# Joining the half-filled products of a routed feed-forward, and moving steps around its expert tiles

## What is computed

```python
logits = x @ W_router.T                      # 8 experts, top 2 per token
probs = softmax(logits); rw, sel = top_k(probs, 2)
combine = zeros((T, E)).at[arange(T)[:, None], sel].add(rw)
sh = silu_and_mul(x @ Ws_gate_up, 704) @ Ws_down          # shared expert: 256 -> 2*704 -> 256
shared_out = sh * sigmoid(x @ W_sgate.T)
gu = einsum('th,ehi->eti', x, We_gate_up)                 # each expert: 256 -> 2*176
# ... silu_and_mul(gu, 176), then We_down: 176 -> 256, weighted with combine, plus shared_out
```

## Time and profile before

| what | us |
|---|---|
| median of 3 runs (1372.93 to 1376.32) | 1374.88 |
| the profiled execution, its own time | 1379.76 |
| its span, first to last instruction | 1377.8 |
| TensorE busy in the span | 1289.3 (94%) |
| VectorE, ScalarE, GpSimd busy | 888.4, 776.2, 436.3 |
| last stage, from its first instruction at 1161.3 | 216.5 |

### The profile page before, as it was taken

How to read it: one execution, slowest core, us unless ns; L and a number is a source line. 1 busy time by engine, 2 the same in 40 slices (tenths; PEclk the granted TensorE clock), 3 DMA queues, 4 the chain that set the end, 5 groups by cost and what they waited for, 6 DMA issues and landing times. The chain is left out here.

```text
span 1377.8 us, 23715 instructions
## 1 busy us (share of the span) xinstructions
PE 1289.3 (94%) x8242; PEld 1139.5 (83%) x8242; DVE 888.4 (64%) x2436; ACT 776.2 (56%) x2113; POOL 436.3 (32%) x420
## 2 busy tenths in 40 slices
PE   3799999999999879999999988999999998899998
PEld 3588888888888768888888877998988987789986
DVE  4688888888887656643433345667676767585647
ACT  3587777777777623322222257666666665455542
POOL 1365556545654433100000002222241332053430
PEclk8999999999999979999999989999999999899999
DMA  7000000000000400300000020000000024123433
GB/s 251 9 1 1 9 1 0 0 8 0 0 0 1 98 0 1 123 1 0 0 0 1 9 69 9 1 9 1 9 29 4 13 83 115 43 73 102 124 113 136
DMA packets 42771, 49.91 MB, mean 36 GB/s; under 512 B 13711, under 2 KB 35160, under 8 KB 41912
## 3 DMA queue, kind: packets, MB, share of 16 engines
q1 hardware_dynamic: 38888, 38.33, 9.2%
q0 software_dynamic: 3792, 10.40, 2.0%
HBM read 36.23 MB, written 12.49 MB: 35 GB/s over the span
## 5 line engine op out<-in xcount | busy, mean ns | idle before, releaser
L955 POOL TENSOR_TENSOR probs_a<-probs_a,rden_a 128x512 f32<-128x512 f32 x128 | 133.4, 1042 | 337.1 <-DVE rden_a L914 335.4
L96 PE MATMUL bank<-wvo_hi,pc_hi_a 128*128 128x256 f32 x512 | 153.7, 300 | 1.9 <-DVE pc_lo_a L921 1.9
L1308 ACT ACTIVATE act_g_f<-bank 128x512 f32<-128x512 f32 x64 | 38.3, 599 | 189.1 <-PE bank L98 189.1
L97 PE MATMUL bank<-wvo_lo,pc_hi_a 128*128 128x256 f32 x512 | 143.9, 281 | 0.0
L98 PE MATMUL bank<-wvo_hi,pc_lo_a 128*128 128x256 f32 x512 | 143.9, 281 | 0.0
L826 ACT ACTIVATE pc_hi_a<-bank 128x512 fp32r<-128x512 f32 x128 | 76.6, 599 | 107.1 <-PE bank L98 105.0
L1365 DVE TENSOR_TENSOR hid_f<-act_g_f,bank 128x512 f32<-128x512 f32 x64 | 44.0, 687 | 143.3 <-ACT act_g_f L1308 143.3
L817 ACT ACTIVATE probs_a<-bank,nbias_a,q_r_a 128x128 f32<-128x128 f32 x256 | 114.5, 474 | 21.5 <-DVE nbias_a L908 21.5
L917 DVE TENSOR_TENSOR pt_lo_a<-bank,pt_hi_a 128x512 fp32r<-128x512 f32 x128 | 87.7, 686 | 58.8 <-ACT pt_hi_a L823 58.1
L921 DVE TENSOR_TENSOR pc_lo_a<-bank,pc_hi_a 128x512 fp32r<-128x512 f32 x128 | 88.0, 688 | 45.5 <-ACT pc_hi_a L826 45.5
L96 PE MATMUL bank<-xt_hi_f,w_gu_hi_f 128*128 128x512 f32 (+1 forms) x256 | 101.9, 398 | 0.0
(11 more groups left out here) (292 smaller groups left out, 4017.5 us busy)
## 6 DMA issues: line engine op xcount, KB each, us to landing
xs_raw_f<-rows_in SPq DMA_DIRECT2D x39, 129.0 KB
q_raw_p<-in_L_xattn_Wq SPq DMA_DIRECT2D x4, 1024.0 KB, 8.8
y_tok_f<-rows_out SPq DMA_DIRECT2D x4, 1024.0 KB, 8.9
we_raw<-in_L_ffn_We_gate_up SPq DMA_DIRECT2D x2, 1408.0 KB, 12.0
o_raw_p<-in_L_xattn_Wo SPq DMA_DIRECT2D x1, 2048.0 KB, 10.3
x_sb<-in_x SPq DMA_DIRECT2D x4, 512.0 KB, 13.8
ctx_raw_a<-in_ctx SPq DMA_DIRECT2D x8, 256.0 KB, 2.8
o_early<-in_L_xattn_Wo SPq DMA_DIRECT2D x1, 2048.0 KB, 15.4
```

Source lines behind the costliest of these rows:

```text
L96: nc.tensor.matmul(out, w[0], x[0], start=start, stop=False)
L97: nc.tensor.matmul(out, w[0], x[1], start=False, stop=False)
L955: nc.gpsimd.tensor_tensor(probs[:, i % 2, :, :], probs[:, i % 2, :, :], scale, ALU.mult).then_inc(sem("probs_scaled"), 1)
```

## The change

In the layer-1 feed-forward and the loads for it:

- The shared expert's weights lie so that the last 64 gate and 64 up columns are neighbours; `GU` of slot 5 becomes one product of 128 output rows, gate in rows 0 to 63 and up in rows 64 to 127 of `g_bank` (6 matmuls in place of 12). The load of these weights becomes four DMAs, two of them of 64-column pieces.
- `D m 5`: the low part of the 64 hidden rows is written to rows 64 to 127 of the high tile, and the down weights are loaded twice; two matmuls over 128 rows take the place of three over 64.
- `DN`: 176 rows as 128 + 48; the 48 rows and their low parts are stacked at rows 0 and 64 of a 112-row operand: 3 + 2 matmuls in place of 3 + 3. DVE writes a second copy of 48 columns of `e_hid`, and splits `HT` in two instructions.
- The order: `SD`, `SE`, `SX` later and spread, `SX 6`, `SX 7` in the first tiles; `XT 0` into slot 14 ahead of `D 2 0`; `X 3 0`, `X 3 1` out of slot 10 and into tiles 8 and 9; `CB 3 1` out of slot 23 and behind `D 3 5`.
- SP loads the experts' down weights only after the fourth `GU`; it stores the last group in two halves, and `E m 0` waits for the first half of `D m 5` only.

```diff
-        dma.dma_start(self.ws_raw[:, :, :], a["L1_ffn_Ws_gate_up"].rearrange("(k c) n -> c k n", c=P)).then_inc(self.loaded, 16)
+        shared = a["L1_ffn_Ws_gate_up"].rearrange("(k c) n -> c k n", c=P)
+        for half in range(2):
+            dma.dma_start(self.ws_raw[:, :, half * FULL:(half + 1) * FULL], shared[:, :, half * I_SH:half * I_SH + FULL]).then_inc(self.loaded, 16)
+            dma.dma_start(self.ws_raw[:, :, 2 * FULL + half * REST:2 * FULL + (half + 1) * REST],
+                          shared[:, :, half * I_SH + FULL:(half + 1) * I_SH]).then_inc(self.loaded, 16)
...
-        return [slice(half * I_SH + i * P, half * I_SH + min((i + 1) * P, I_SH)) for half in range(2)]
+        return [slice(2 * FULL, 2 * I_SH)] if i == SLOTS - 1 else [slice(half * FULL + i * P, half * FULL + (i + 1) * P) for half in range(2)]
...
-        0: ["NB 3 0", "NB 3 1", "NB 3 2", "NB 3 3", "SD 0", "SD 1", "SC 2 0", "SC 2 1", "SC 2 2", "SC 2 3"],
-        1: ["NX 3 0", "NX 3 1", "SD 2", "SD 3", "SD 4", "SD 5", "SE 0"],
-        2: ["X 1 0", "X 1 1", "RT 3", "SE 1"],
-        3: ["RL 3", "SE 2"],
+        0: ["NB 3 0", "NB 3 1", "NB 3 2", "NB 3 3", "SC 2 0", "SC 2 1", "SC 2 2", "SC 2 3"],
+        1: ["NX 3 0", "NX 3 1", "SD 0", "SD 1", "SD 2"],
+        2: ["X 1 0", "X 1 1", "RT 3", "SD 3", "SD 4", "SD 5"],
+        3: ["RL 3", "SE 0", "SE 1"],
         4: ["RS 3", "RQ 3 0"],
-        5: ["RQ 3 1", "SE 3"],
-        6: ["RK 3", "SE 4"],
-        7: ["PL 3 0", "PL 3 1", "SC 3 0", "SC 3 1", "SC 3 2", "SC 3 3", "SE 5"],
+        5: ["RQ 3 1"],
+        6: ["RK 3", "SE 2", "SE 3"],
+        7: ["PL 3 0", "PL 3 1", "SC 3 0", "SC 3 1", "SC 3 2", "SC 3 3", "SE 4"],
         8: ["TB 0"],
-        9: ["X 2 0", "X 2 1", "SE 6"],
-        10: ["X 3 0", "X 3 1", "SE 7"],
-        11: ["SX 0", "SX 1", "SX 2"],
-        12: ["SX 3", "SX 4"],
-        13: ["SX 5", "SX 6", "SX 7"],
+        9: ["X 2 0", "X 2 1", "SE 5"],
+        10: ["SE 6", "SE 7"],
+        11: ["SX 0"],
+        12: ["SX 1", "SX 2"],
+        13: ["SX 3", "SX 4"],
+        14: ["SX 5"],
...
+        if s == AHEAD - 1:
+            out += steps("XT 0")
         if i >= 2:
             out += steps(f"D {m} {i - 2}")
...
-    order += steps("XT 0")
...
+        order += steps(*(["SX 6"], ["SX 7"])[j]) if j < 2 else []
+        order += steps(f"X {LAST} {j - 8}") if j in (8, 9) else []
...
-    order += finish(LAST) + steps(f"E {LAST} 0", f"E {LAST} 1")
+    order += finish(LAST) + steps(f"CB {LAST} 1", f"E {LAST} 0", f"E {LAST} 1")
...
+            sp.wait_ge(sem("up_filled"), 4)
+            sp.dma_start(de_raw[:, 0, :, :], down[0:P]).then_inc(sem("de_loaded"), 16)
...
+            for half in range(2):
+                sp.wait_ge(sem("out_freed"), 2 * G - 1 + half)
+                store(LAST * GB + 2 * half, 2)
...
+                            pe.wait_ge(sem("up_freed" if half or (s - 2) % SLOTS == SLOTS - 1 else "gate_freed"), s - 1)
...
+                            nc.tensor.matmul(out_of(b), hs[0][:, s % 3, toks], ds[0][:, i, :], start=False, stop=False)
+                            last = nc.tensor.matmul(out_of(b), hs[0][:, s % 3, toks], ds[1][:, i, :], start=False, stop=b % 2 == 1)
+                            if b == 1:
+                                last.then_inc(sem("half_down"), 1)
...
+                    three_pass(nc, out, [v[:, j % 2, 0:P] for v in ht], [v[:, 0, own] for v in de_flat], True, False)
+                    nc.tensor.matmul(out, ht[0][0:STACK, j % 2, P:2 * P], de_flat[0][0:STACK, 1, own], start=False, stop=False)
+                    last = nc.tensor.matmul(out, ht[0][0:STACK, j % 2, P:2 * P], de_flat[1][0:STACK, 1, own], start=False, stop=True)
...
+                    ups = u_bank[s % 2][:, :] if r == P else g_bank[s % 2][DUP:DUP + r, :]
...
+                    nc.vector.tensor_tensor(e_hid[:, j % 2, 0:I_MOE], e_act[:, j % 2, :], g_bank[j % 2][:, I_MOE:2 * I_MOE], ALU.mult)
+                    nc.vector.tensor_tensor(e_hid[:, j % 2, P + DUP:P + STACK], e_act[:, j % 2, P:I_MOE], g_bank[j % 2][:, I_MOE + P:2 * I_MOE],
+                                            ALU.mult).then_inc(sem("e_hid_ready"), 1)
...
+                    nc.vector.tensor_tensor(ht[1][:, j % 2, 0:P], u_bank[j % 2][:, 0:P], f32(ht[0][:, j % 2, 0:P]), ALU.subtract)
+                    twin = ht[0][DUP:STACK, j % 2, P:2 * P]
+                    nc.vector.tensor_tensor(twin, u_bank[j % 2][DUP:STACK, P:2 * P], f32(twin), ALU.subtract).then_inc(sem("ht_ready"), 1)
```

More of the change, by code:

```diff
@@ L50 @@
 I_SH, I_MOE, E = 704, 176, 8
+REST = I_SH % P
+FULL = I_SH - REST
 NF0 = 2048
@@ L1404 @@
 SLOTS = 6
-EI = I_MOE // 2
+DUP = 64
+TAIL = I_MOE - P
+STACK = DUP + TAIL
 TOGETHER = 3
@@ L1759, in _ @@
             sp.dma_start(ds_raw[:, 0:full, :], shared[0:full * P].rearrange("(t p) d -> p t d", p=P)).then_inc(sem("ds_loaded"), 16)
-            sp.dma_start(ds_raw[0:tail, full, :], shared[full * P:I_SH]).then_inc(sem("ds_loaded"), 16)
-            for c in range(2):
-                sp.dma_start(de_raw[0:EI, c, :, :], a["L1_ffn_We_down"][:, c * EI:(c + 1) * EI, :].rearrange("e p d -> p e d")).then_inc(sem("de_loaded"), 16)
+            for lane in (0, DUP):
+                sp.dma_start(ds_raw[lane:lane + tail, full, :], shared[full * P:I_SH]).then_inc(sem("ds_loaded"), 16)
+            down = a["L1_ffn_We_down"].rearrange("e p d -> p e d")
+            sp.wait_ge(sem("up_filled"), 4)
+            sp.dma_start(de_raw[:, 0, :, :], down[0:P]).then_inc(sem("de_loaded"), 16)
+            for lane, rows in ((0, TAIL), (TAIL, DUP - TAIL), (DUP, TAIL)):
+                sp.dma_start(de_raw[lane:lane + rows, 1, :, :], down[P:P + rows]).then_inc(sem("de_loaded"), 16)
             sp.wait_ge(sem("table_ready"), 1)
@@ L1782, in _, with store @@
                 sp.dma_start(y_tok[m], by_token[:, m * GB:(m + 1) * GB, :]).then_inc(sem(f"y_back{m}"), 16)
[L1783 to L1790, removed]
+            def store(first, batches):
+                sp.dma_start(out_dram[first:first + batches].rearrange("b s d -> s b d"), core.x[:, first:first + batches, :]).then_inc(sem("stored"), 16)
+            for m in range(LAST):
+                sp.wait_ge(sem("combined"), m + 1)
+                store(m * GB, GB)
+            for half in range(2):
+                sp.wait_ge(sem("out_freed"), 2 * G - 1 + half)
+                store(LAST * GB + 2 * half, 2)
+            sp.wait_ge(sem("stored"), 16 * (G + 1))
         @block.tensor
@@ L1819, in _ @@
                         pe.wait_ge(sem("y_ready"), TILES - 1 + s - AHEAD)
[L1820 removed]
+                    for half, (bank, cols) in enumerate(zip((g_bank[s % 2], u_bank[s % 2]), gate_up.columns(i))):
                         if s >= 2:
[L1822 to L1823 removed]
+                            pe.wait_ge(sem("up_freed" if half or (s - 2) % SLOTS == SLOTS - 1 else "gate_freed"), s - 1)
                         for k in range(KD):
[L1825 removed]
+                            last = three_pass(nc, bank[:, :], [v[:, k, cols] for v in ws], [xt_of(p, k, m) for p in range(2)],
                                               k == 0, k == KD - 1)
@@ L1871, in _ @@
                         pe.wait_ge(sem("y_ready"), j - 1)
-                    for c in range(2):
-                        last = nc.tensor.transpose(u_bank[j % 2][0:EI, c * P:(c + 1) * P], e_hid[:, j % 2, c * EI:(c + 1) * EI], core.ident[:, :])
+                    for c, rows in enumerate((P, STACK)):
+                        last = nc.tensor.transpose(u_bank[j % 2][0:rows, c * P:(c + 1) * P], e_hid[:, j % 2, c * P:c * P + rows], core.ident[:, :])
                     last.then_inc(sem("ht_filled"), 1)
@@ L1879, in _ @@
                         pe.wait_ge(sem("de_split"), E)
-                    for c in range(2):
-                        last = three_pass(nc, u_bank[j % 2][:, D:2 * D], [v[0:EI, j % 2, c * P:(c + 1) * P] for v in ht],
-                                          [v[0:EI, c, bass.ds(experts[j] * D, D)] for v in de_flat], c == 0, c == 1)
+                    out, own = u_bank[j % 2][:, D:2 * D], bass.ds(experts[j] * D, D)
+                    three_pass(nc, out, [v[:, j % 2, 0:P] for v in ht], [v[:, 0, own] for v in de_flat], True, False)
+                    nc.tensor.matmul(out, ht[0][0:STACK, j % 2, P:2 * P], de_flat[0][0:STACK, 1, own], start=False, stop=False)
+                    last = nc.tensor.matmul(out, ht[0][0:STACK, j % 2, P:2 * P], de_flat[1][0:STACK, 1, own], start=False, stop=True)
                     last.then_inc(sem("dn_filled"), 1)
@@ L1910, in _ @@
                     if e == 0:
-                        act.wait_ge(sem("de_loaded"), 32)
-                    nc.scalar.activation(de[0][0:EI, :, e, :], de_raw[0:EI, :, e, :], ACT.Copy).then_inc(sem("de_hi"), 1)
+                        act.wait_ge(sem("de_loaded"), 64)
+                    part = (slice(0, STACK if e % 2 else P), e % 2, slice(e // 2 * 2, e // 2 * 2 + 2), slice(None))
```

(1 more changed line is left out.)

36 lines of the change are left out of this document (21 added, 15 removed), and 2 rows, old and new, of the table extras.

## The result

| | before | after |
|---|---|---|
| median of the runs, us | 1374.95 | 1365.52 (1364.07 to 1367.74, 6 runs) |
| the profiled execution, its own time | 1379.76 | 1365.47 |
| span of its trace | 1377.8 | 1363.4 |
| TensorE busy in the span, us | 1289.3 | 1273.6 |

What follows compares the result with a forecast made beforehand. TensorE was taken as busy nearly throughout, with waits and POOL's scatters binding before the tiles; -9.3 + 0.4 - 3.6 - 5.4 + 0.3 = -17.6 us gave a median of 1357.3, range 1352 to 1366 with the first two rivals.

Steps and rivals of the forecast that it cites:

- The sum carried over whole from the profiled execution to the median: Whole kernel: the -17.6 us reckoned on the profiled execution (1379.76) applied in full to the median (1374.88), giving 1357.3.
- Rival 1: Slots 0 to 7: the pause stays or was mostly the profiled execution's own; 1363.8 us, chance 0.26.
- Part 1: Slots 0 to 7, up to `PL 3`: shorter wait, faster clock, fewer products, less a small delay; -9.3 us.
- the -4.1 for a clock that stays up: Behind the wait ahead of `RT 3`: the shorter wait leaves TensorE's clock up in place of half; -4.1 us, otherwise 0.
- `GU 5` and `D 0 5`, -2.3: Slots 0 to 7: products removed from these two steps, and changes of row height avoided; together -2.3 us.
- the +0.5 for two `SE` in slot 3: Slot 3: two `SE` beside table loads make ACT late for `A 4`, so `D 0 3` waits; +0.5 us, bounds 0 and 1.0.
- Part 2: `PL 3` to the first tile: POOL's scatters set the pace, saved products count at nothing, slow clock costs; +0.4 us.
- Part 3: The 39 tiles: one product less each (-4.7), against uncovered `X 3` (+0.8) and `HT` transposes (+0.3); -3.6 us.
- `SX 6` and `SX 7` hide behind the fill of the first tiles: First tiles: these two moved steps were expected to be covered, with no cost entered in the sum.
- Part 4: Slots 15 to 23 and the end: fewer products, shorter tail and a last store half as large; -5.4 us.
- Part 5: Loads before the stage: three more DMAs issued ahead of the experts' weights; +0.3 us, bounds 0 and +1.1.
- The rival of DVE's pace: Tiles: held twin instructions make DVE's chain longer than the tile; +19.9 us in place of -3.6, 1380.8, chance 0.04.

Runs made afterwards that it cites:

- e2: The changed kernel with joined products, divided loads and half stores, but every other step and the down-weight load back in its old place; median 1364.84 us, ratio 0.9923 to before.
- e3: The kernel before with only the changed kernel's order of steps and later load of the experts' down weights; median 1374.82 us, ratio 1.0001.
- e1: The kernel before, unchanged, run again for a second profiled execution; median 1375.16 us, ratio 0.9995.
- e5: The kernel before, unchanged, run once more for a third trace; the traced execution took 1379.15 us.
- e11: The kernel before with one edit, the experts' down weights loaded only from the fourth `GU` on; median 1374.21 us, ratio 0.9987.
- e4: The changed kernel with `SX 5`, `SX 6` and `SX 7` done earlier, in slots 13 and 14 before the tiles; 1362.79 us, ratio 0.9911 to before.
- e6: The changed kernel, unchanged, run again for a second trace; measured 1364.89 us.
- e7: e4 with slots 15 and 16 moved ahead of the tiles, `SX` and `CB` steps shifted; 1359.13 us, ratio 0.9891 to before.
- e8: The changed kernel with one more product, its result overwritten, in each of the 39 tiles; 1367.93 us, ratio 0.9947 to before.
- e12: e7 with the tables read into registers 2 tiles at a time in place of 3; 1357.04 us, ratio 0.9869 to before.

## Why the prediction was partly right

The sign held, and half of the mechanism: TensorE's products. They were 10.4 of the 17.6 us and the half store 0.5, and e2 shows 9.8 to 10.1 for the two. The other 6.7 were to come from the order, above all from a wait and a slow clock that go, and e3 shows 0. The size was too large by 8.2 us. The range held by 0.5 us, and by its rivals alone: the bounds of the forecast's own parts ended at 1361. By its own steps:

- **The sum carried over whole from the profiled execution to the median.** This failed, 4.8 us. Rival 1, the pause being that execution's own, came nearest: 1363.8 against 1365.5. e1 and e5 show 2 of the 4.3 us as chance. What is left, 1.3 us of wait and a longer slow stretch behind it, stands in every trace of before and in neither e3 nor e11, whose traces are 3.0 and 1.8 us shorter from S to the end than e1's; yet in the ratios it is worth 0 (at most 1.2 by e3's interval) and 1.8 us (0 to 3.4 by e11's). The likeliest reading is that most executions don't have it, and that the traced ones do. That is argued, not shown: of the other executions there is no trace, and whether tracing makes the load late stays open.

  The table holds a second reading that fits as well. Where the first slot runs at half clock, old and new order are alike: S to `RT 3` is 14.2 us in e2 and 14.2 in e4, S to SC 42.3 and 42.4 (the first trace of after was slow there for longer and has 15.3). Where it runs at the full clock, the old order has 14.3 to 14.6 (e1, e5) and the new one 12.8 (e3, e6), and the slow stretch behind `RT 3` is longer in the old one. All three traces of before are of the second kind. If most other executions are of the first, the order gives them nothing; no run tells which kind is the commoner.

  The clock has a part in e5's excess in any case: its mean granted clock is 0.975, and the five other executions of before with 0.975 took 1376.0 to 1379.1 us. That of the first trace, 0.978, is the commonest of all, and the 23 others with it took 1372.9 to 1377.3, so its 1379.76 is not the clock's.
- **Part 1, -9.3, measured -6.7.** The wait ahead of `RT 3` went to 1.0 (forecast 0.9). The step that failed is the -4.1 for a clock that stays up. In after it does stay up there but is low behind the barrier instead, in e6 it falls behind `RT 3` in spite of the short wait. A shorter wait goes with a shorter slow stretch, it did not take it away: behind 4.3 us of wait the mean clock from 1175 to 1190 is 0.66 (some 10 us slow), behind the 2.2 of e1 and e5 0.77 (some 7), and in e6 only 3 to 4 us are slow. `GU 5` and `D 0 5`, -2.3: between e3 and e6, alike in order, S to SC differs by 1.4; 0.6 of what is missing is a wait for `hs_lo` ahead of `D 0 3` that e3 does not have, where the +0.5 for two `SE` in slot 3 was expected. But e3 has the same two `SE`, so they alone are not its cause; what is stays open.
- **Part 2, +0.4, measured -0.2.** TensorE waits 4.6 us ahead of `XT 0` (forecast 5.7); 0.9 of the difference is that `XT 0` now starts 28.51 us behind `SC 3` in place of 29.37, as its rows came sooner. That the savings of this stretch count at nothing was right, and e7 shows the other side: work put under the scatters is worth 3.7 us.
- **Part 3, -3.6, measured -2.2.** The -2.2 hangs on the traces: against e1 and e5, which ran at half clock at the first tile for some 7 us where the first trace of before did for 3 to 4, it would be -3.2 and -3.3. The product at 0.12 us in each of 39 tiles was mis-sized: 3.4 us in place of 4.7, because every third tile goes by the read of registers (e8, e12). "`SX 6` and `SX 7` hide behind the fill of the first tiles" failed: 1.4 to 1.7 us (e4). `X 3` cost 0.7 for the 0.8 forecast (e3). The transposes of `HT` cost nothing: ordinary tiles went from 2.11 to 2.00, the product's 0.12. DVE is busy 1.72 us a tile (41.29 of 50.51 us in 24 tiles of e6), above my 1.65, and doesn't set the pace.
- **Part 4, -5.4, measured -5.2.** GU to the first product of `GU 23` -2.4 (forecast -2.3). From there to the last store's issue 10.57 became 8.5: -2.0, of which `GU 23` is 1.4, so the shorter tail gave 0.6 where I had 1.2 (1.5 less 0.3). In the traces e3 has -0.5 here and e2 -4.7, of which 3.9 is products and 0.8 the half store. The half store gave 0.8, forecast 0.5.
- **Part 5, +0.3, measured -0.2:** nothing that can be seen, also with 256-byte pieces. S varies by several us from trace to trace, so this rests on means: 1161.9 in the five traces with the old loads, 1161.8 in the nine with the new. By the Trainium skill, DMA: Bandwidth & Descriptors, Specifications, they are below the 512 bytes that the full rate wants; S did not come later for it by anything that these means can tell.

The last store's two issues, after:

```profile
1360.04 1.16 SPq L1801 DMA_DIRECT2D out<-x_sb  x2
```

The second begins 0.37 us, the length of one, ahead of 1361.20, at 1360.83. The tail's missing 0.6 is DVE, which in slots 22 and 23 has no idle time. In after, `D 3 4` waits 1.2 us where it waited 0.6 before. TensorE, then VectorE:

```profile
1356.60 0.39 PE L98 MATMUL bank<-ds_hi_f,hs_hi_f 128*128 128x256 f32 x1 [1.23 <-DVE hs_lo_f L1982]
```

```profile
1355.25 0.69 DVE L2034 TENSOR_TENSOR hid_f<-act_g_f,bank 64x512 f32<-64x512 f32 x1
1355.87 0.68 DVE L1982 TENSOR_TENSOR hs_lo_f<-hid_f,hs_hi_f 128x512 fp32r<-128x512 f32 x1
1356.64 0.69 DVE L1982 TENSOR_TENSOR hs_hi_f<-hid_f,hs_hi_f 64x512 fp32r<-64x512 f32 x1
1357.36 1.67 DVE L2101 SCALAR_TENSOR_TENSOR x_sb<-y_tok_f,gate_w_r,x_sb 128x256 f32<-128x256 f32 x4
1359.13 1.66 DVE L2060 SCALAR_TENSOR_TENSOR x_sb<-bank,gate_s_r,x_sb 128x256 f32<-128x256 f32 x4
```

The rival of DVE's pace rested on held instructions. VectorE in a tile of after:

```profile
1315.71 0.34 DVE L2082 TENSOR_TENSOR e_hid_f<-e_act_f,bank 128x176 f32<-128x176 f32 x1 [0.20 <-ACT e_act_f L1962]
1315.96 0.20 DVE L2083 TENSOR_TENSOR e_hid_f<-e_act_f,bank 128x48 f32<-128x48 f32 x1
1316.08 0.28 DVE L2088 TENSOR_TENSOR ht_lo_f<-bank,ht_hi_f 128x128 fp32r<-128x128 f32 x1
1316.38 0.29 DVE L2090 TENSOR_TENSOR ht_hi_f<-bank,ht_hi_f 48x128 fp32r<-48x128 f32 x1
```

The second and third start before the one ahead has ended (0.25 and 0.12 us behind its start); the fourth, whose operands begin at partition 64, starts 0.02 us after the end of the third, 0.30 behind its start. The Trainium skill, VectorE: DVE Perf Modes, section Two Vector instructions with no wait between them, has an instruction that starts in another group of 32 partitions held until every earlier Vector instruction has finished; the trace agrees. By these starts it costs some 0.1 us a tile, an estimate, and is far from binding, and in the tiles of e6 from 1260 to 1315 us TensorE waits for no other engine at all. So the rival of DVE's pace is out, by the trace.

## What to carry to other kernels

A profiled execution is one draw: before a stall in it is priced, set its time against the median of the plain runs, and count the excess against the stalls first, the unnamed ones above all. A product that is taken out of a loop is worth its price only in the turns that TensorE paces; look at the turns one by one, not at their mean (here 2.11, 2.11, 2.29 hid a third with another limit). And work moved under a wait for a chain on another engine is a gain of its own: 3.7 us here, four tenths of what all the joined products gave.
